# Turning the residual with VectorE and memory instead of TensorE, with the FFN products half a step later

## The chip, the cores and the metric

One core of a Trainium2 chip runs the whole program in one launch. The metric is device time in microseconds (us), the median of several runs. TensorE (PE) does the matmuls, VectorE (DVE), ScalarE (ACT) and GpSimd (POOL) the elementwise work, and SyncE (SP) issues nearly all DMAs.

## The reference

x is 4 x 2048 x 512, fp32. The function is one transformer layer: attention with a causal linear recurrence of 16 heads of 32, then a feed-forward part with low-rank factors. Cut to what matters:

```
x = layernorm(x);  xn = layernorm(x) * ln_g + ln_b
q, k, v = split(xn @ W_qkv + b_qkv);  gate = sigmoid(x @ W_gate + b_gate);  gate /= mean(gate)
q, k = relu(q*gate)**2 + eps, relu(k*gate)**2 + eps
kv[t] = kv[t-1] + k[t] v[t]^T;  ks[t] = ks[t-1] + k[t];  o[t] = (q[t] kv[t]) / (q[t] ks[t] + eps)
x1 = x + o @ W_proj + b_proj
P = layernorm(x1) @ U1;  H = gelu(P @ V1 + b1);  Q = H @ U2;  out = x1 + Q @ V2 + b2
```

U1 is 512 x 128, V1 128 x 2048, U2 2048 x 128, V2 128 x 512.

## The kernel before

The rows of x are cut into 64 chunks of 128 rows (one of the four batches after another at each of 16 positions), and the kernel is a list of 64 steps and a few at the end, written out by `steps(step)` for each engine. In a step (p, b) three chunks are at work: n = chunk b does its projections, c = chunk b-1 its attention and output projection, d = chunk b-2 enters the feed-forward part. Every fp32 product is made of three matmuls, hi by hi, hi by lo and lo by hi (`product`, L849 to L851), so each operand is split by a copy to fp32r (hi) and a subtraction (lo).

The feed-forward part works on groups of two chunks (256 rows), one group for two steps. An odd step (b odd) has the product with U1 (12 matmuls of 256 columns, L959), and pairs 0 to 3 of the eight pairs of 128-row blocks of the hidden layer; the even step that follows has pairs 4 to 7. A pair is an `h_pair` on TensorE (P by V1, 6 matmuls), a `gelu` on ScalarE (L530), an `h_head` on VectorE (the cast h_hi, L665), an `h_tail` on GpSimd (h_lo, L447), and a `q_pair` on TensorE (H by U2, 6 matmuls, added up in ps_q). The odd step also has the result of the group before (`result`, Q by V2).

TensorE's order in a step is: gate; turn of c's queries (`transpose4`, L856); key; turn of d's residual; result (odd only); query; U1 product (odd) or two h pairs (even); scores of c (L980, from key_t and query_t); value; two h pairs (odd only); state of c (L999); outputs of c (L1010, L1016); key sums of n (L1026); two h pairs; y of c (output projection); four q pairs.

VectorE's: gate out of PSUM (L691), gate scale, keys (L653, L656, [x1t_lo L683], L660), results (L716, odd), queries (same lines), pt_lo (L726, odd), block transpose of the keys into zs (L737), probs = scores times the causal mask (L741), values (L749), statistics of a later chunk (L597, L603), state (L767) among two h_heads, ot_lo (L773), zt_lo (L620), two h_heads, key_sums and the denominators (L791 to L805), x1 and its statistics (L815 to L822), zs = normalised x1 (L830), qt_lo (L834, even).

The keys of a chunk are turned without TensorE: VectorE's instruction turns each 32 x 32 block where it stands (L737), SP stores the tile to `blocks_dram` (L351), and four loads of 64 KB, in pieces of 32 elements, put the blocks in their places in `key_t` (L359). The residual of chunk d is in zs; TensorE turns it with four transposes against the identity (L941) into the PSUM bank ps_t, ScalarE copies x1t_hi out (L551) and VectorE makes x1t_lo (L683). The queries are turned in the same way (L926), and stay so.

SP's queue works in the order in which it is written: store results (odd), key_blocks, turned_rows (the means, 4 bytes a row), the four key_t loads, rows, carry_rows, key_sums, xs, xt. It waits at each item for its semaphore, and later items wait behind.

## Time and profile before

| | |
|---|---|
| median of 3 runs | 1702.19 us (1701.56 to 1702.4) |
| the profiled execution | 1701.4 us |
| its span, first to last instruction | 1699.7 us |
| busy: TensorE, VectorE, GpSimd, ScalarE | 1668.6, 1437.1, 880.5, 629.6 us |
| granted TensorE clock, mean | 0.998 |
| chain that ended last | 93% TensorE, 3% VectorE |

Busy time is the union of an engine's instructions. A matmul's shown length (0.39 us for 512 columns) is longer than the distance to the next one, since they overlap: the time that work takes on TensorE is read from the starts.

### The profile page before, as it was taken

How to read it: one execution, taken by the hardware profiler on the slowest of the kernel's cores; microseconds unless marked ns; L12 is line 12 of the kernel's file. 1: busy time of each engine (PE TensorE's matmuls, PEld its weight loads, DVE VectorE, ACT ScalarE, POOL GpSimd, SP SyncE). 2: the span in 40 equal slices, each digit the busy share in tenths (PEclk: the TensorE clock that was granted, in tenths of full speed). 3: DMA queues.
4: the chain of work that ended last, by engine and by line, in shares of the span. 5: the costliest groups of instructions: out<-in, count | busy, mean ns of one | idle time of the engine just before them, and what ended most of it. 6: DMA issues, size and time to landing. Idle time of an engine off the chain costs nothing.

```text
span 1699.7 us, 39613 instructions
## 1 busy us (share of the span) xinstructions
PE 1668.6 (98%) x16221; PEld 1404.5 (83%) x16221; DVE 1437.1 (85%) x2223; ACT 629.6 (37%) x1178; POOL 880.5 (52%) x1026
## 2 busy tenths in 40 slices
PE   6899999999999999999999999999999999999997
PEld 4688888888888888888888888888888888888886
DVE  6888888888888888888888888888888888888885
ACT  4233334333433433433433333333333334334333
POOL 3355555555555555555555555555555555555540
PEclk9999999999999999999999999999999999999999
DMA  8323333333332233242243233333323333323310
GB/s 224 93 58 64 65 75 46 70 75 57 71 70 47 74 71 60 73 64 53 74 72 58 74 46 70 75 59 70 73 45 73 70 60 73 71 47 72 60 45 26
DMA packets 206324, 115.67 MB, mean 68 GB/s; under 512 B 151144, under 2 KB 161792, under 8 KB 206144
## 3 DMA queue, kind: packets, MB, share of 16 engines
q1 hardware_dynamic: 205280, 111.57, 31.6%
q8 instruction: 129, 2.11, 0.7%
q10 hardware_dynamic: 864, 1.57, 0.4%
q14 instruction: 51, 0.42, 0.2%
HBM read 79.38 MB, written 33.72 MB: 67 GB/s over the span
## 4 chain that ended last, share of the span: by engine, by line
PE 93%; DVE 3%; DMA 1%; issue 1%; SPq 1%; ACT 0%; POOL 0%; DVEq 0%; POOLq 0%
PE ps_a L849 11%; PE ps_a L850 10%; PE ps_a L851 10%; PE scores L849 8%; PE scores L851 8%; PE scores L850 8%; PE ps_h L849 4%; PE ps_h L850 4%; PE ps_h L851 4%; PE scores L980 4%; PE scores L1016 4%; PE ps_q L849 3%; PE ps_q L850 3%; PE ps_q L851 3%; PE scores L856 3%; PE scores L1010 2%
## 5 line engine op out<-in xcount | busy, mean ns | idle before, releaser
L447 POOL TENSOR_TENSOR h_lo<-h_full,h_hi 128x512 fp32r<-128x512 f32 x244 | 318.0, 1309 | 233.7 <-DVE h_hi L665 233.7
L849 PE MATMUL ps_a<-wx_hi,zt_hi 128*128 128x512 f32 x768 | 315.7, 411 | 6.6 <-DVE key_sums L787 4.2
L850 PE MATMUL ps_a<-wx_lo,zt_hi 128*128 128x512 f32 x768 | 305.1, 397 | 0.0
L851 PE MATMUL ps_a<-wx_hi,zt_lo 128*128 128x512 f32 x768 | 305.1, 397 | 0.0
L530 ACT ACTIVATE h_full<-ps_h,cols 128x256 f32<-128x256 f32 x512 | 204.0, 475 | 149.7 <-PE ps_h L851 149.6
L665 DVE CAST h_hi<-h_full 128x512 fp32r<-128x512 f32 x256 | 193.5, 766 | 22.9 <-ACT h_full L530 15.8
L849 PEld LDWEIGHTS ps_a<-wx_hi,zt_hi 128*128 128x128 f32 x768 | 145.3, 189 | 43.4 <-DVE zt_lo L620 7.4
L851 PEld LDWEIGHTS ps_a<-wx_hi,zt_lo 128*128 128x128 f32 x768 | 145.1, 189 | 35.6
L850 PEld LDWEIGHTS ps_a<-wx_lo,zt_hi 128*128 128x128 f32 x768 | 145.3, 189 | 28.7 <-issue 0.5
L541 ACT ACTIVATE query_t<-scores 128x512 f32<-128x512 f32 x64 | 38.3, 598 | 345.4 <-PE scores L856 345.4
L401 POOL TENSOR_TENSOR small<-moments,eps_col 128x1 f32<-128x1 f32 x64 | 12.2, 190 | 278.6 <-DVE moments L822 278.6
L849 PE MATMUL ps_h<-pt_hi,v_hi 128*128 128x256 f32 x512 | 144.2, 282 | 1.4 <-DVE pt_lo L726 0.9
L741 DVE TENSOR_TENSOR probs<-scores,causal 128x2048 f32<-128x2048 f32 x64 | 144.1, 2251 | 1.4 <-PE scores L980 1.4
L849 PE MATMUL ps_q<-h_hi,u_hi 128*128 128x256 f32 x512 | 144.8, 283 | 0.4
L850 PE MATMUL ps_h<-pt_lo,v_hi 128*128 128x256 f32 x512 | 144.2, 282 | 0.0
L851 PE MATMUL ps_q<-h_hi,u_lo 128*128 128x256 f32 x512 | 143.7, 281 | 0.0
L850 PE MATMUL ps_q<-h_lo,u_hi 128*128 128x256 f32 x512 | 143.7, 281 | 0.0
L467 POOL TENSOR_TENSOR key_lo<-keys,key_hi 128x512 fp32r<-128x512 f32 x64 | 85.3, 1332 | 112.4 <-ACT key_hi L561 112.4
L851 PE MATMUL ps_h<-pt_hi,v_lo 128*128 128x256 f32 x512 | 143.2, 280 | 0.0
L463 POOL TENSOR_TENSOR keys<-keys,eps_col 128x512 f32<-128x512 f32 x64 | 66.6, 1041 | 123.9 <-DVE keys L660 123.9
L401 POOL TENSOR_TENSOR small<-small,minus_half 128x1 f32<-128x1 f32 x192 | 119.8, 624 | 15.1
L849 PE MATMUL scores<-wx_hi,zt_hi 128*128 128x512 f32 x256 | 106.7, 417 | 0.0
(156 smaller groups left out, 4133.2 us busy)
## 6 DMA issues: line engine op xcount, KB each, us to landing
xs<-L_attn_x SPq DMA_DIRECT2D x64, 256.0 KB, 4.1
key_blocks<-zs SPq DMA_DIRECT2D x64, 256.0 KB, 2.0
key_t<-key_blocks SPq DMA_DIRECT2D x256, 64.0 KB
out<-x1s SPq DMA_DIRECT2D x64, 256.0 KB, 2.1
xt<-x_turned SPq DMA_DIRECT2D x63, 256.0 KB, 4.2
key_sums<-carry_rows SPq DMA_DIRECT2D x60, 256.0 KB, 3.8
rows<-turned_rows SPq DMA_DIRECT2D x63, 64.0 KB, 4.5
x1s<-L_attn_W_gate SPq DMA_DIRECT2D x4, 256.0 KB, 4.1
```

The source lines that it names most:

```text
L401: E.tensor_tensor(out_, a, b, op).then_inc(sem_, 1)
L447: E.tensor_tensor(h_lo[:, i % SLOTS, :], h_full[:, i % SLOTS, :], h_hi[:, i % SLOTS, :].bitcast(F32), ALU.subtract).then_inc(s["h_lo_ready ...
L463: E.tensor_tensor(keys[:, n.half, :], keys[:, n.half, :], eps_wide, ALU.add)\
L467: E.tensor_tensor(key_lo[:, :], keys[:, n.half, :], key_hi[:, :].bitcast(F32), ALU.subtract).then_inc(s["key_lo_ready"], 1)
L530: last = E.activation(h_full[:, i % SLOTS, a * GROUP:(a + 1) * GROUP], ps_h[i % 2][:, a * GROUP:(a + 1) * GROUP], ACT.Gelu_apprx_tanh, bia ...
L665: E.tensor_copy(h_hi[:, i % SLOTS, :], h_full[:, i % SLOTS, :]).then_inc(s["h_hi_ready"], 1)
L741: E.tensor_tensor(probs[:, :, :].rearrange("p j (k t) -> p (j k) t", k=KT), scores[:, :].rearrange("p (g t) -> p g t", g=blocks), causal.u ...
L849: E.matmul(ps, wh, mh, start=start and i == 0, stop=False)
L850: E.matmul(ps, wh, ml, start=False, stop=False)
L851: mm = E.matmul(ps, wl, mh, start=False, stop=stop and i == last)
L980: mm = E.matmul(ps_scores[j][:, ft * P:(ft + 1) * P], key_t[rows, ft, :], query_t[rows, ft, :], start=True, stop=True, tile_position=(HEAD ...
L1016: mm = E.matmul(ps_scores[j][ft * HEAD:(ft + 1) * HEAD, 0:P], values[:, c.half, h * HEAD:(h + 1) * HEAD], probs[:, j, ft * P:(ft + 1) * P] ...
```

## The change

The turn of the residual leaves TensorE and PSUM. VectorE turns zs by 32 x 32 blocks into the queries' buffer right after the gate has left PSUM; SP, first thing in its step, stores that to a new tensor in memory, `res_dram`, waits, and sends four loads back into zs. ScalarE makes x1t_hi from zs, ahead of ot_hi in an odd step and after the last gelu in an even one; VectorE makes x1t_lo ahead of ot_lo in an odd step and after the denominators in an even one. The queries of chunk n wait for that store. The block transpose of the keys now goes to the gate's buffer, and the denominators, which use that buffer, wait for `blocks_out`.

The FFN products are placed anew. The U1 product comes after the key sums of the odd step, and h pairs 0 and 1 at its end. The even step has h pairs 2 and 3 after the gate product, q pairs 0 to 3 with h pairs 4 and 5 after the query product, h pairs 6 and 7 before y, and q pairs 4 to 7 last. The gelus, the h_heads (0 to 3 in a row after the gate) and the h_tails follow.

```
SP, first in its step:
+                d = Chunk(p, b - 2)
+                if d.exists:
+                    sp.wait_ge(s["res_ready"], d.done())
+                    for j in range(HPG):
+                        wait(sp, res_in[j], d.done(16, 16) - 16)
+                    sp.dma_start(res_dram, queries[:, :]).then_inc(s["res_out"], 16)
+                    sp.wait_ge(s["res_out"], d.done(16, 16))
+                    for j in range(HPG):
+                        sp.dma_start(zs[j * HEAD:(j + 1) * HEAD, :].rearrange("d (f a t) -> d f a t", f=KT, t=HEAD),
+                                     res_dram.rearrange("(a d) (f j t) -> j d f a t", d=HEAD, f=KT, t=HEAD)[j])\
+                            .then_inc(res_in[j], 16)
-                    sp.dma_start(blocks_dram, zs[:, :]).then_inc(s["blocks_out"], 16)
+                    sp.dma_start(blocks_dram, gate[:, :]).then_inc(s["blocks_out"], 16)
GpSimd:
+                early_tails = ffn.exists and b % 2 == 0 and not is_last(p)
+                if early_tails:
+                    for i in range(4):
+                        h_tail(ffn, i)
...
+                if early_tails:
+                    add_bias_out()
+                    add_bias(n)
ScalarE:
+                def turned_residual():
+                    if d.exists:
+                        for j in range(HPG):
+                            act.wait_ge(res_in[j], d.done(16, 16))
+                        E.activation(x1t_hi[:, :, d.half * P:(d.half + 1) * P],
+                                     zs[:, :].rearrange("p (k n) -> p k n", k=KT), ACT.Copy)\
+                            .then_inc(s["x1t_hi_ready"], 1)
VectorE:
+                def early_heads():
+                    if ffn.exists and b % 2 == 0:
+                        for i in range(4):
+                            h_head(ffn, i, finishing)
+                def turn_residual():
+                    if d.exists:
+                        dve.wait_ge(s["z1_ready"], d.done())
+                        if c.exists:
+                            dve.wait_ge(s["tq_done"], c.done())
+                        E.transpose(queries[:, :], zs[:, :]).then_inc(s["res_ready"], 1)
...
+                    turn_residual()
+                    early_heads()
...
+                    if d.exists:
+                        dve.wait_ge(s["res_out"], d.done(16, 16))
                     squared_relu(n, s["query_done"], s["query_steps"], ps_a, QUERY, queries[:, :])
...
-                    E.transpose(zs[:, :], keys[:, n.half, :]).then_inc(s["blocks_ready"], 1)
+                    E.transpose(gate[:, :], keys[:, n.half, :]).then_inc(s["blocks_ready"], 1)
...
+                if b % 2:
+                    x1t_tail()
...
+                    dve.wait_ge(s["blocks_out"], n.done(16, 16))
...
+                if b % 2 == 0:
+                    x1t_tail()
TensorE:
+                if ffn.exists and b % 2 == 0:
+                    h_pair(ffn, 2)
+                    h_pair(ffn, 3)
...
-                    transpose4(zs, s["tx_done"])
...
+                    if d.exists:
+                        pe.wait_ge(s["state_ready"], d.done())
+                    for i in range(4):
+                        q_pair(ffn, i)
+                    h_pair(ffn, 4)
+                    h_pair(ffn, 5)
...
-                if ffn.exists and b % 2:
-                    h_pair(ffn, pairs[0])
-                    h_pair(ffn, pairs[1])
...
+                if b % 2 and ffn.exists:
...
+                    pe.wait_ge(s["x1t_ready"], d.done())
+                    wait(pe, s["h_full_ready"], Group(ffn.p, ffn.off - 1).done(PAIRS, PAIRS))
+                    product(ps_h[1][:, 0:GROUP], [(u1_hi[:, k, :], u1_lo[:, k, :]) for k in range(KT)],
+                            [(x1t_hi[:, k, :], x1t_lo[:, k, :]) for k in range(KT)]).then_inc(s["p_done"], 1)
+                if ffn.exists and b % 2 == 0:
+                    h_pair(ffn, 6)
+                    h_pair(ffn, 7)
...
+                if ffn.exists and b % 2:
+                    h_pair(ffn, 0)
+                    h_pair(ffn, 1)
+                if ffn.exists and b % 2 == 0:
...
+                    for i in range(4, 8):
                         q_pair(ffn, i)
```

## Rows read from the trace of the kernel before

**Rows 1.** Windows: length, busy of PE, PEld, DVE, ACT, POOL, clock, DMA share, GB/s

```profile
807.54:834.68 27.14, 27.14 (x265) 23.15 (x264) 23.45 (x36) 9.64 (x18) 13.96 (x17) 1.00 0.35 75
834.68:859.05 24.37, 24.37 (x247) 20.48 (x246) 20.71 (x32) 9.64 (x18) 13.78 (x17) 1.00 0.35 55
```

**Rows 2.** Waits, 400 to 1600 us, TensorE's largest (total, times, longest)

```profile
PEld scores L1016 <- issue: 9.3, 47, 0.2
```

**Rows 3.** Timeline of TensorE around the residual's turn: start, length, instruction

```profile
810.76 0.60 PE L856 MATMUL scores<-ident,zs 128*128 128x128 f32 x4
811.12 0.48 PE L849 MATMUL scores<-v_hi,pt_hi 128*128 128x512 f32 x1
811.43 0.39 PE L850 MATMUL scores<-v_lo,pt_hi 128*128 128x512 f32 x1
```

**Rows 4.** Windows of TensorE alone: query, U1, scores, value, state with outputs and sums

```profile
812.60:815.39 2.79, 2.79 (x14) 1.00 0.68 231
815.39:816.81 1.42, 1.42 (x13) 1.00 0.72 270
816.90:818.00 1.10, 1.10 (x33) 1.00 0.24 93
818.00:820.91 2.91, 2.91 (x17) 1.00 0.24 90
822.42:824.85 2.43, 2.43 (x100) 1.00 0.07 7
```

**Rows 5.** Timeline of VectorE in the same odd step

```profile
811.23 0.75 DVE L653 SCALAR_TENSOR_TENSOR keys<-scores,small,bias 128x512 f32<-128x512 f32 x1
...
815.66 0.75 DVE L653 SCALAR_TENSOR_TENSOR queries<-ps_a,small,bias 128x512 f32<-128x512 f32 x1
...
818.18 0.70 DVE L737 STREAM_TRANSPOSE zs<-keys 128x512 f32<-128x512 f32 x1
818.80 2.25 DVE L741 TENSOR_TENSOR probs<-scores,causal 128x2048 f32<-128x2048 f32 x1
821.11 0.75 DVE L749 SCALAR_TENSOR_TENSOR values<-ps_a,small,bias 128x512 f32<-128x512 f32 x1
...
822.69 0.43 DVE L665 CAST h_hi<-h_full 128x512 fp32r<-128x512 f32 x1
...
823.42 1.34 DVE L665 CAST h_hi<-h_full 128x512 fp32r<-128x512 f32 x1
```

**Rows 6.** Timeline of SP's queue: xt, and key_t behind turned_rows and without it

```profile
811.55 0.43 SPq L285 DMA_DIRECT2D xt<-x_turned  x1
...
823.13 3.25 SPq L359 DMA_DIRECT2D key_t<-key_blocks  x4
...
1619.07 2.61 SPq L359 DMA_DIRECT2D key_t<-key_blocks  x4
```

**Rows 7.** DMA issues: count, KB each, median us from issue to landing

```profile
key_blocks<-zs SPq DMA_DIRECT2D x64, 256.0 KB, 2.0
...
xt<-x_turned SPq DMA_DIRECT2D x63, 256.0 KB, 4.2
```

**Rows 8.** DMA view, 811 to 818 us: busy tenths in 40 slices

```profile
DMA  0001354445777499999974320006999999930000
```

**Rows 9.** The same view, 1619 to 1625 us

```profile
DMA  0000000001797169742599237873000100000000
```

**Rows 10.** The same view, 823 to 835 us

```profile
DMA  0110000422403959950010435302000096319000
```

**Rows 11.** Timeline at the end: the last zs, its split and its U1 product

```profile
1674.24 0.55 DVE L830 TENSOR_SCALAR zs<-x1s,moments,small 128x512 f32<-128x512 f32 x1 [0.93 <-POOL small L401]
...
1675.54 0.60 ACT L551 ACTIVATE x1t_hi<-scores 128x512 fp32r<-128x512 f32 x1 [0.64 <-PE scores L856]
...
1676.17 0.69 DVE L683 TENSOR_TENSOR x1t_lo<-scores,x1t_hi 128x512 fp32r<-128x512 f32 x1 [0.81 <-ACT x1t_hi L551]
...
1676.92 0.38 PE L849 MATMUL ps_h<-x1t_hi,u_hi 128*128 128x256 f32 x1
```

More of the change, by code:

```diff
@@ L215, in block_kernel @@
         xt_in = [sem(f"xt_in{i}") for i in range(4)]
+        res_in = [sem(f"res_in{j}") for j in range(HPG)]
         key_t_in = [sem(f"key_t_in{j}") for j in range(HPG)]
@@ L469, in step @@
                 center(Chunk(p, b + 1))
-                if ffn.exists and not is_last(p):
-                    h_tail(ffn, pairs[0])
-                    h_tail(ffn, pairs[1])
-                    h_tail(ffn, pairs[2])
-                    h_tail(ffn, pairs[3])
+                if early_tails:
+                    for i in range(4, 8):
+                        h_tail(ffn, i)
                 if c.exists:
@@ L537, in step @@
                 ffn = Group(p, (b - 3) // 2) if b % 2 else Group(p, (b - 4) // 2)
-                pairs = range(4) if b % 2 else range(4, 8)
+                def turned_residual():
[6 more added lines that the diff above has]
+                if ffn.exists and b % 2 == 0:
+                    gelu(ffn, 2)
+                    gelu(ffn, 3)
+                if n.exists:
+                    act.wait_ge(s["gate_evac"], n.done())
+                    E.activation(gate[:, :], gate[:, :], ACT.Sigmoid, accum_out=gate_sum[:, :])\
+                        .then_inc(s["gate_sig"], 1)
                 if c.exists:
@@ L675, in step @@
                 ffn = Group(p, (b - 3) // 2) if b % 2 else Group(p, (b - 4) // 2)
-                pairs = range(4) if b % 2 else range(4, 8)
                 finishing = is_last(p)
@@ L768, in step @@
                                     ALU.add).then_inc(s["state_ready"], 1)
-                if ffn.exists and b % 2:
-                    h_head(ffn, pairs[1], finishing)
+                if b % 2:
+                    x1t_tail()
                 if c.exists:
@@ L775, in step @@
                 z_tail(Chunk(p, b + 1))
-                if ffn.exists:
-                    h_head(ffn, pairs[2], finishing)
-                    h_head(ffn, pairs[3], finishing)
+                if b % 2 and ffn.exists:
+                    dve.wait_ge(s["pt_hi_ready"], ffn.done())
+                    E.tensor_tensor(pt_lo[:, :], ps_h[1][:, 0:GROUP], pt_hi[:, :].bitcast(F32), ALU.subtract)\
+                        .then_inc(s["pt_ready"], 1)
+                if ffn.exists and b % 2 == 0:
+                    h_head(ffn, 6, finishing)
+                    h_head(ffn, 7, finishing)
                 if n.exists:
@@ L908, in step @@
                 result = Group(p, (b - 5) // 2) if b % 2 else None
-                pairs = range(4) if b % 2 else range(4, 8)
                 if n.exists:
@@ L952, in step @@
                     project(QUERY, ps_a, s["query_done"])
-                if b % 2 and ffn.exists:
-                    if isinstance(p, int) and p == 0:
-                        pe.wait_ge(s["stage_lo"], len(tiles))
-                    pe.wait_ge(s["x1t_ready"], d.done())
-                    wait(pe, s["h_full_ready"], Group(ffn.p, ffn.off - 1).done(PAIRS, PAIRS))
-                    product(ps_h[1][:, 0:GROUP], [(u1_hi[:, k, :], u1_lo[:, k, :]) for k in range(KT)],
-                            [(x1t_hi[:, k, :], x1t_lo[:, k, :]) for k in range(KT)]).then_inc(s["p_done"], 1)
-                if ffn.exists and b % 2 == 0:
-                    h_pair(ffn, pairs[0])
-                    h_pair(ffn, pairs[1])
+                if ffn.exists and b % 2 == 0:
+                    if d.exists:
[4 more added lines that the diff above has]
+                    h_pair(ffn, 5)
                 if c.exists:
@@ L989, in step @@
                     project(VALUE, ps_a, s["value_done"])
-                if ffn.exists and b % 2:
-                    h_pair(ffn, pairs[0])
-                    h_pair(ffn, pairs[1])
                 if c.exists:
@@ L1038, in step @@
                             [(wp_hi[:, k, :], wp_lo[:, k, :]) for k in range(KT)]).then_inc(s["y_done"], 1)
-                if ffn.exists:
+                if ffn.exists and b % 2:
+                    h_pair(ffn, 0)
+                    h_pair(ffn, 1)
+                if ffn.exists and b % 2 == 0:
                     if c.exists:
                         pe.wait_ge(s["state_ready"], c.done())
-                    for i in pairs:
+                    for i in range(4, 8):
                         q_pair(ffn, i)
@@ L1070 @@
     blocks_dram = nc.dram_tensor("key_blocks", (P, DM), _mybir.dt.float32, kind="Internal").ap()
+    res_dram = nc.dram_tensor("residual_blocks", (P, DM), _mybir.dt.float32, kind="Internal").ap()
     rows_dram = nc.dram_tensor("turned_rows", (BATCHES, P), _mybir.dt.float32, kind="Internal").ap()
-    block_kernel(nc, *args, out, carry_dram, rows_dram, blocks_dram)
+    block_kernel(nc, *args, out, carry_dram, rows_dram, blocks_dram, res_dram)
     r = _run(nc, [arrays], core_ids=[0])
```

93 lines of the change are left out of this document (32 added, 61 removed).

## The prediction

> **What bounds the kernel now.** I read the share of each engine over one odd and one even step first, then the table of waits, then the order of work inside one odd step, engine by engine. The two windows [rows 1] run from the turn of the queries in one step to the same point in the next: TensorE is busy for all of 27.14 us in the odd step and all of 24.37 in the even one. A pair of steps is 51.51 us. The waits on TensorE's side between 400 and 1600 us are only small ones put down to "issue" [rows 2], so no other engine holds it up. VectorE is busy 23.45 and 20.71 us of the same windows: second, but not far behind. TensorE's granted clock is 1.00, the 2.4 GHz level, in both windows. So what leaves TensorE is gained only if the engines behind it keep the new, shorter pace, and the question is asked step by step, because the change also makes the two kinds of step unequal.
>
> **What leaves TensorE.** The four turns of zs, once a step. Their slot is 810.76 to 811.12, 0.36 us, and the product behind them needs 0.31 to its second matmul where 0.23 is the pace (2.79 us for twelve) [rows 3, 4]; 0.43 us a step, 0.86 a pair. The Trainium skill (TensorE: Matmul & The Clock Gate, Part 4: PE-mode transpose) gives about 275 ns for a turn inside a kernel, which by its figure would be 1.1 us a step, an estimate of 70 us for the kernel. The trace has 0.60 us for four that overlap, and the slot in it is what counts.
>
> **What moves.** A half of the second-factor work (four q pairs) and two h pairs go from the odd to the even step. A product of twelve 256-column matmuls takes 1.42 us [rows 4], a pair has six, 0.71. So six pairs are 4.26 us. TensorE's own work becomes 27.14 - 0.43 - 4.26 = 22.45 in the odd step and 24.37 - 0.43 + 4.26 = 28.20 in the even step, 50.65 together: if all is covered, 0.86 us a pair is gained.
>
> **The odd step, walked through.** I keep the clock of the step that begins at 807.54. Without the turns the query product (2.79) ends at 815.0. The product with U1, that stood behind it (1.42), is now after the sums. So the scores run 815.1 to 816.2 (1.10), the value product to 819.1 (2.91), and the state products to 819.65 (some 0.46 of the 2.43 us that they, the output products and the sums take together) [rows 4]. There the output products want probs.
>
> VectorE cannot be so early. It takes the queries out of PSUM when their product is done and then has its chain: from 815.66 to the start of probs at 818.80 are 3.14 us, of which 0.34 is pt_lo, which moves away; and probs takes 2.25 [rows 5]. From 815.3 (VectorE reaches it at 814.7 to 815.3, since keys at 811.23 and what follows move up by the x1t_lo that leaves, and get the new transpose in the time that it spent waiting for the gate) that makes 815.3 + 2.80 + 2.25 = 820.35, 0.75 late. Before, two h pairs and the U1 product (2.84) lay in TensorE's way to this point and covered it.
>
> The second place is the U1 product. TensorE without waits would be at it at 819.65 + (2.43 - 0.46) = 821.6 [rows 4]. It needs x1t_lo, which VectorE now makes behind values, the statistics and the state: 1.58 from values to the end of the statistics [rows 5], some 0.4 for the state (an estimate: a quarter of the columns of values), 0.69 for itself [rows 11]; 820.4 + 2.7 = 823.1. So by here the odd step is 1.5 us late in all (the 0.75 is in it). Behind it the y product (its ot_lo is made by 823.8) and h pairs 0 and 1 (pt_lo while y runs) are covered; nothing gives the 1.5 back.
>
> **The transfers.** The turned residual leaves from the queries' buffer, and the queries may not be written before it has left. SP reaches the new store only behind xt, issued at 811.55 [rows 6], so at 812.0. Alone a store of this size lands 2.0 us later [rows 7], at 814.0, which would be in time. But key_sums, xs and xt are in flight and their packets keep the DMA engines at 7 to 9 tenths up to about 814.8 [rows 8]; xt lands 4.2 us after its issue [rows 7], at 815.75, and the two result stores behind it fill 1.3 us, 815.75 to 817.05 [rows 8], 0.65 each. In order behind xt the store lands at 816.35. VectorE wants the buffer at 815.3: 1.05 us late, with 0 (store alone) as the lower bound. I take 1.05, as the rows show queued transfers there. It delays queries and probs alike, and so adds to the 1.5: 2.55 a pair. In the even step the transposed residual is ready later and the early heads lie ahead of the queries: covered.
>
> The four loads into zs are of the kind of key_t: 128-byte packets. Where no turned_rows store is ahead of them, their packets are through by about 1623.8, 4.7 us after the first issue [rows 6, 9]; behind turned_rows they last to some 833.4, 10.3 us [rows 6, 10]. The new ones go behind a big store, so I take the short form: 816.35 + 4.7 = 821.1 to 822, ScalarE's copy 0.6 [rows 11], done before VectorE's 822.4. Covered, by little. If they take 10.3 it is the rival below. key_blocks is sent about a microsecond later in the step than now, when SP has issued the four loads (816.35 + 3.25 = 819.6); its reader is in the next step. It goes out of the gate buffer, which is written again only at the denominators.
>
> **The even step.** VectorE's work is 20.71 busy plus 0.62 for the transpose (818.18 to 818.80) plus four heads of 0.43 (port free) to 1.34 us (GpSimd in its own subtraction) [rows 5], 1.7 to 5.4; with the 3.66 us in which it was not busy in this step [rows 1] that is 26.7 to 30.4 against TensorE's 28.2. Early heads come in pairs that slip through between GpSimd's tails, so I take about 3.8 for the four: 28.8, and the waits among the 3.66 shrink (the gate's sigmoid of up to 1.7 is now covered). I put nothing down for it and keep up to 2.2 for the range.
>
> **The end.** The last residual has no next step to hide in. Now zs is written at 1674.24 to 1674.79 and the U1 product starts at 1676.92 [rows 11], 2.1 us. After: transpose 0.7, store 2.0 and 0.3 to notice it, loads 4.7, copy 0.6, x1t_lo 0.69, and some 0.1 between each: 9.3. Plus 7. If the loads are of the long form it is 5.6 more.
>
> **Sum.** 31 full pairs. -0.86 x 31 = -27; +2.55 x 31 = +79; +7 at the end. 1701.4 + 59 = 1760; the median of the runs shown is 1702.2, so the same figure stands for it. With the store alone (0 instead of 1.05) it is 1728.
>
> **Rivals.**
> 1. All covered: TensorE keeps the pace, 1701.4 - 27 + 7 = 1681. For it: TensorE has no wait now, VectorE is under 90%. Against: the chain query, probs, output is counted from rows and is longer than what TensorE has left beside it; it decides if VectorE gets from the query product to probs' end in less than 4.6 us.
> 2. A draw: the delays in the odd step are only about the 0.86 gained, 1700 to 1705.
> 3. The residual's loads take as long as key_t's now. They land at 816.35 + 10.3 = 826.7, ScalarE stands at its wait with ot_hi behind it, x1t_lo is ready at 828.1 instead of 824.1: 4.0 a pair more, +124, 1885. It sets in when the loads take over 6.5 us. The Trainium skill (DMA: Bandwidth & Descriptors, the table at its head) wants 512 B a descriptor for line rate, which speaks against any plan with 128-byte pieces; both kinds of rows above have them, so it does not choose between 4.7 and 10.3.
> 4. VectorE becomes the bound of the even step too: +2.2 x 31 = +68, 1828. The Trainium skill (SBUF — State Buffer, Who interferes with whom) says that a copy of VectorE in its fast mode and a GpSimd instruction exclude each other for their whole length. By that rule, the trace agrees: 1.34 against 0.43 for the same cast.
>
> **Chances.** The odd step's delays outweigh the gain (1706 to 1810): 0.61. All or nearly all covered: 0.16. Draw: 0.06. Slow loads: 0.07. Even step too: 0.10. Range 1690 to 1810: it leaves out most of rival 1 and rival 3 and a part of rival 4; the likeliest case alone is 1725 to 1790. No change can be told from one of 0.2%, 3.4 us. Faster 0.16, same 0.06, slower 0.78.
>
> **What would show it.** In the trace after: TensorE waiting at the output products for probs, at the value product for queries, and at the U1 product for x1t_lo, all in odd steps, each around 1 us; VectorE waiting for a DMA into residual_blocks ahead of the queries; pairs of about 53.2 us; even steps near 28.2; ScalarE with a short or no wait for zs. The forecast is wrong if odd steps are 22.5 long (VectorE quicker than counted), if ScalarE waits for zs by 4 us and more, or if VectorE never idles in the even steps and these are 30 long.

## The result, and the profile after

| | before | after |
|---|---|---|
| median (runs, range) | 1701.9 us (4, 1701.6 to 1702.4) | 1845.0 us (4, 1835.4 to 1855.1) |
| ratio, 95% interval | | 1.083 (1.080 to 1.086) |
| profiled execution, its span | 1701.4, 1699.7 us | 1855.1, 1853.3 us |
| a pair of steps, behind the first | 51.51 us, always | 54.3 to 60, mean 56.0 us |
| last turn of the queries to the end | 42.8 us | 57.9 us |

The change is a loss of 8.3%: 85 us more than forecast, and 35 above the upper end of the range. The four runs stand in two pairs, near 1836 and near 1854 us, and the profiled one is the longest, so the trace below has 154 us to explain where the medians have 143. Three parts make the 154 us between the two spans: 8 us up to the fifth turn of the queries, 130 us from there to the last one, 15 us at the end. The page of the kernel after shows the change of character first: the engines' busy times, and the chain that ended last, which was 93% TensorE before.

```profile
PE 1694.7 (91%) x15965; PEld 1402.0 (76%) x15965; DVE 1511.8 (82%) x2291; ACT 625.5 (34%) x1178; POOL 921.7 (50%) x1022
...
DMA 49%; DVE 26%; PE 14%; issue 5%; SPq 5%; ACT 1%; DVEq 0%; POOL 0%; POOLq 0%; ACTq 0%
...
residual_blocks<-queries SPq DMA_DIRECT2D x64, 256.0 KB, 4.8
zs<-residual_blocks SPq DMA_DIRECT2D x256, 64.0 KB, 2.5
```

VectorE is busy for 75 us more, of which its 64 new transposes of 0.70 explain 45; GpSimd is busy for 41 us more with four instructions fewer. Something makes instructions longer. The two windows that answer to [rows 1], an odd step and the even one behind it:

```profile
916.47:944.64 28.17, 25.70 (x238) 20.77 (x237) 20.72 (x35) 7.34 (x15) 10.07 (x18) 0.94 0.41 89
944.64:972.58 27.94, 26.84 (x268) 22.91 (x267) 25.47 (x35) 11.79 (x22) 19.33 (x17) 1.00 0.37 69
```

From turn to turn TensorE's own work is 23.87 us odd (the 22.45 of the forecast, which counts from gate to gate, with the 1.42 of two h pairs) and 26.78 even. The odd step has 4.3 us over that, the even one 1.2. TensorE is no longer busy throughout, and in the odd step its granted clock is 0.94. The waits between 400 and 1600 us, to be held against [rows 2]:

```profile
ACT x1t_hi L564 <- DMA zs<-residual_blocks: 126.8, 21, 7.7
...
DVE queries L682 <- DMA residual_blocks<-queries: 68.2, 38, 3.5
...
PE scores L1031 <- DVE probs L776: 53.5, 33, 2.4
...
PE ps_a L885 <- DVE queries L682: 29.1, 15, 2.7
```

Two chains hold TensorE: the queries wait for the store in nearly every step (38 of 43), and the output products wait for probs in odd and even steps alike. Added up by kind of step, TensorE's matmuls wait 2.5 us in an odd step and 1.5 us in an even one, on the mean between 400 and 1600 us.

**The odd step.** SP's queue first ([rows 6] show xt before), then VectorE ([rows 5]):

```profile
921.35 0.43 SPq L286 DMA_DIRECT2D xt<-x_turned  x1
921.96 0.33 SPq L348 DMA_DIRECT2D residual_blocks<-queries  x1
926.76 2.62 SPq L351 DMA_DIRECT2D zs<-residual_blocks  x4
```

```profile
926.82 0.75 DVE L682 SCALAR_TENSOR_TENSOR queries<-ps_a,small,bias 128x512 f32<-128x512 f32 x1 [3.30 <-DMA residual_blocks<-queries]
927.61 0.75 DVE L685 SCALAR_TENSOR_TENSOR queries<-queries,gate_scale,gate 128x512 f32<-128x512 f32 x1
928.39 0.69 DVE L689 SCALAR_TENSOR_TENSOR queries<-queries 128x512 f32<-128x512 f32 x1
929.00 0.70 DVE L772 STREAM_TRANSPOSE gate<-keys 128x512 f32<-128x512 f32 x1
929.63 2.25 DVE L776 TENSOR_TENSOR probs<-scores,causal 128x2048 f32<-128x2048 f32 x1
```

The store lands 4.8 us after its issue, and VectorE stands 3.30 us before it touches the queries. From there to probs it takes 2.81 us, which is the 2.80 of the forecast. So it is, within 0.1 us, in 13 of the 21 odd steps; in the other 8 (most of them between 1140 and 1490 us) it takes 3.0 to 4.8 us, and there TensorE waits up to 2.35 us for probs instead. TensorE's value product, which writes the bank that the queries are read from, waits:

```profile
927.63 0.74 PE L885 MATMUL ps_a<-wx_hi,zt_hi 128*128 128x512 f32 x1 [2.47 <-DVE queries L682]
```

Behind such a wait comes the second loss. This window of the same step shows the granted clock at 0.50, the 1.2 GHz level, while TensorE is busy all the time:

```profile
927.72:931.13 3.41, 3.41 (x8) 2.67 (x9) 3.38 (x4) 0.00 (x0) 0.00 (x0) 0.50 0.64 134
```

It issues 8 matmuls in 3.41 us there, where the 2.4 GHz level has 0.23 us for each. Such a stretch is called a fall below. The whole trace has 27 of them, 108.5 us together (before: 2, 9.6 us, none between 400 and 1600). Each of the 16 between 400 and 1600 us begins 1.8 to 4.0 us behind the start of a wait of TensorE's matmuls of 1.9 to 2.6 us; 9 more waits of 1.8 us and over had none behind them. At half the rate 108.5 us cost at most 54, and at most 49 more than the falls of before.

**The even step.** Here the forecast put nothing down. VectorE's chain, and GpSimd beside it:

```profile
953.64 0.75 DVE L682 SCALAR_TENSOR_TENSOR queries<-ps_a,small,bias 128x512 f32<-128x512 f32 x1 [0.40 <-DMA residual_blocks<-queries]
954.42 1.71 DVE L685 SCALAR_TENSOR_TENSOR queries<-queries,gate_scale,gate 128x512 f32<-128x512 f32 x1
956.17 1.67 DVE L689 SCALAR_TENSOR_TENSOR queries<-queries 128x512 f32<-128x512 f32 x1
957.76 0.70 DVE L772 STREAM_TRANSPOSE gate<-keys 128x512 f32<-128x512 f32 x1
958.39 2.25 DVE L776 TENSOR_TENSOR probs<-scores,causal 128x2048 f32<-128x2048 f32 x1
```

```profile
954.31 1.28 POOL L475 TENSOR_TENSOR x1s<-x1s,bias_out 128x512 f32<-128x512 f32 x1
955.55 1.74 POOL L450 TENSOR_TENSOR xs<-xs,bias_proj 128x512 f32<-128x512 f32 x1
957.25 1.74 POOL L490 TENSOR_TENSOR key_lo<-keys,key_hi 128x512 fp32r<-128x512 f32 x1
```

The same two multiplications of the queries take 1.71 and 1.67 us in place of 0.75 and 0.69, so the chain is 4.75 instead of 2.81. Their ends show how: 954.42 + 1.71 = 956.13 is 0.54 behind the end of GpSimd's addition (954.31 + 1.28 = 955.59), and 956.17 + 1.67 = 957.84 is 0.55 behind the next one's (957.29). VectorE's instruction gets through only when GpSimd's is over, and GpSimd's next one, held in turn, takes 1.74 instead of 1.28. In this step TensorE waits 1.10 us at the output products for probs.

The price could have been read before. In the kernel before, the same engines meet at another place (groups of VectorE, 400 to 1600 us: busy time, mean ns of one):

```profile
L794 DVE SCALAR_TENSOR_TENSOR gate<-queries,key_sums 128x512 f32<-128x512 f32 x46 | 59.1, 1286 | 1.6
L660 DVE SCALAR_TENSOR_TENSOR queries<-queries 128x512 f32<-128x512 f32 x47 | 32.5, 692 | 1.6
```

Both have two tensors of SBUF as inputs. The first runs beside GpSimd's h_tails and takes 1.29 us on the mean; the second ran beside nothing and took 0.69. The Trainium skill (SBUF — State Buffer, Who interferes with whom) says that a VectorE instruction with two SBUF inputs contends with a GpSimd instruction that reads SBUF, and that the later one of them is blocked until the other ends. By that rule, the trace agrees, in both directions. The forecast used the same section for the casts only.

### The profile page after: what moved, and what is told of

Read it like the earlier page. It is cut to its first block, busy times and chain, and to the rows that moved or that the text cites. A ratio compares the mean times of both kernels' runs of the same rounds, so it can differ in the third digit from the quotient of the medians.

```text
span 1853.3 us, 39585 instructions
## 1 busy us (share of the span) xinstructions
PE 1694.7 (91%) x15965; PEld 1402.0 (76%) x15965; DVE 1511.8 (82%) x2291; ACT 625.5 (34%) x1178; POOL 921.7 (50%) x1022
## 3 DMA queue, kind: packets, MB, share of 16 engines
q10 hardware_dynamic: 864, 1.57, 0.3%
## 4 chain that ended last, share of the span: by engine, by line
DMA 49%; DVE 26%; PE 14%; issue 5%; SPq 5%; ACT 1%; DVEq 0%; POOL 0%; POOLq 0%; ACTq 0%
DMA turned_rows<-small 23%; DMA residual_blocks<-queries 15%; DMA carry_rows<-key_sums 11%; DVE probs L776 4%; DVE queries L689 4%; DVE queries L685 3%; DVE queries L682 3%; DVE h_hi L694 2%; PE ps_a L885 2%; DVE stats L626 2%; DVE values L784 2%; PE ps_a L887 2%; PE ps_a L886 2%; DVE gate L772 1%; SPq L283 1%
## 5 line engine op out<-in xcount | busy, mean ns | idle before, releaser
L460 POOL TENSOR_TENSOR h_lo<-h_full,h_hi 128x512 fp32r<-128x512 f32 x240 | 335.4, 1421 | 134.3 <-DVE h_hi L694 134.3
L885 PE MATMUL ps_a<-wx_hi,zt_hi 128*128 128x512 f32 x768 | 320.6, 417 | 54.4 <-DVE queries L682 48.0
L887 PE MATMUL ps_a<-wx_hi,zt_lo 128*128 128x512 f32 x768 | 311.8, 406 | 0.0
L886 PE MATMUL ps_a<-wx_lo,zt_hi 128*128 128x512 f32 x768 | 311.6, 406 | 0.0
L694 DVE CAST h_hi<-h_full 128x512 fp32r<-128x512 f32 x256 | 169.3, 702 | 16.1 <-ACT h_full L551 15.9
L887 PEld LDWEIGHTS ps_a<-wx_hi,zt_lo 128*128 128x128 f32 x768 | 149.1, 194 | 37.1
L886 PEld LDWEIGHTS ps_a<-wx_lo,zt_hi 128*128 128x128 f32 x768 | 149.8, 195 | 31.4 <-issue 0.5
L592 ACT ACTIVATE ot_hi<-scores 128x512 fp32r<-128x512 f32 x64 | 38.4, 599 | 270.8 <-PE scores L1037 270.8
L682 DVE SCALAR_TENSOR_TENSOR queries<-ps_a,small,bias 128x512 f32<-128x512 f32 x64 | 48.0, 750 | 98.9 <-DMA residual_blocks<-queries 96.3
```

The lines of the kernel that those rows point to most:

```text
L460: E.tensor_tensor(h_lo[:, i % SLOTS, :], h_full[:, i % SLOTS, :], h_hi[:, i % SLOTS, :].bitcast(F32), ALU.subtract).then_inc(s["h_lo_ready ...
L682: E.scalar_tensor_tensor(out=dst, in0=ps[:, :], scalar=small[:, n.slot, 4:5], in1=bias[:, group, :], op0=ALU.mult, op1=ALU.add).then_inc(c ...
L694: E.tensor_copy(h_hi[:, i % SLOTS, :], h_full[:, i % SLOTS, :]).then_inc(s["h_hi_ready"], 1)
L885: E.matmul(ps, wh, mh, start=start and i == 0, stop=False)
L886: E.matmul(ps, wh, ml, start=False, stop=False)
L887: mm = E.matmul(ps, wl, mh, start=False, stop=stop and i == last)
```

## The experiments

All ratios are to the kernel before, run beside it on the same chip. The step lengths are from turn to turn of the queries, means between 400 and 1600 us, and falls are the stretches at half clock in the same part, in the profiled execution.

| | edit | median us (range) | ratio, 95% | odd, even step | falls |
|---|---|---|---|---|---|
| | changed kernel | 1845.0 | 1.083 (1.080, 1.086) | 27.46, 28.88 | 16 |
| e1 | residual leaves from another buffer | 1822.3 (1815 to 1824) | 1.069 (1.067, 1.071) | 28.28, 26.78 | 14 |
| e2 | store issued ahead of xs and xt | 1793.3 (1791 to 1797) | 1.053 (1.052, 1.055) | 27.40, 26.77 | 19 |
| e6 | e1 and e2 | 1822.9 (1819 to 1832) | 1.069 (1.067, 1.071) | 28.61, 26.78 | 18 |
| e3 | new FFN placement alone | 1815.6 (1807 to 1821) | 1.064 (1.061, 1.068) | 27.20, 27.73 | 4 |
| e4 | filler products in the waits | 1841.8 (1839 to 1844) | 1.082 (1.080, 1.083) | 27.30, 28.12 | 0 |
| e8 | changed kernel, GpSimd held back | 1809.7 (1804 to 1813) | 1.062 (1.059, 1.064) | 27.17, 27.24 | 8 |
| e5 | e3, GpSimd held back | 1757.9 (1758 to 1760) | 1.032 (1.031, 1.034) | 25.37, 27.73 | 0 |
| e7 | e6, GpSimd held back | 1733.6 (1730 to 1737) | 1.018 (1.016, 1.020) | 25.35, 26.78 | 0 |
| e9 | e7, GpSimd and x1t_lo in a new order | 1719.3 (1717 to 1721) | 1.010 (1.008, 1.011) | 24.69, 26.77 | 0 |
| e12 | e9, keys turned behind values in odd steps | 1710.4 (1709 to 1714) | 1.005 (1.003, 1.006) | 24.54, 26.78 | 0 |
| e10 | before, key_hi ahead of pt_hi | 1723.8 (1722 to 1724) | 1.012 (1.010, 1.014) | 27.93, 24.36 | 0 |
| e11 | before, GpSimd held back | 1701.8 (1700 to 1704) | 1.000 (0.999, 1.001) | 27.14, 24.37 | 0 |

**e1, the store's wait taken away.** The turned residual goes to the half of `values` that is free until the value product of the step, so the queries wait for no store.

```
-                        if c.exists:
-                            dve.wait_ge(s["tq_done"], c.done())
-                        E.transpose(queries[:, :], zs[:, :])
+                        E.transpose(values[:, d.half, :], zs[:, :])
...
-                    if d.exists:
-                        dve.wait_ge(s["res_out"], d.done(16, 16))
                     squared_relu(n, s["query_done"], ...)
...
                     dve.wait_ge(s["value_done"], n.done())
+                    if d.exists:
+                        dve.wait_ge(s["res_out"], d.done(16, 16))
```

> The residual's blocks leave from the half of values that is free at that time, so the queries no longer wait for the store. Theory 1 (that wait is the largest loss of the odd steps, and the fall of TensorE's clock behind it is its second half): VectorE's 96 us of waiting for the store go, odd steps shorten from 26.5-28.2 us to about 25.4, the clock falls in odd steps vanish, 1765 to 1790 us in all against 1845. Theory 2 (VectorE's own chain to probs and x1t_lo is the loss and the store only coincides with it): not under 1825 us.

The time is in neither theory's range. The wait for the store is gone and the even step is at its floor of 26.78, but the odd step grew to 28.28. In the odd step of this kernel the queries start early, and GpSimd's subtraction now falls on them (VectorE's timeline):

```profile
920.86 1.79 DVE L685 SCALAR_TENSOR_TENSOR queries<-queries,gate_scale,gate 128x512 f32<-128x512 f32 x1
922.69 1.66 DVE L689 SCALAR_TENSOR_TENSOR queries<-queries 128x512 f32<-128x512 f32 x1
```

TensorE waits 2.3 us for probs in each of the 22 odd steps, long enough for falls of the clock. The wait for the store had kept the queries out of GpSimd's way: taking it away alone swapped one loss for another.

**e2, the store ahead of xs and xt.** SP issues residual_blocks first and then the loads of xs and xt (whose call stood at the end of the step before).

```
                     sp.dma_start(res_dram, queries[:, :]).then_inc(s["res_out"], 16)
+                load_x(Chunk(p, b + 2))
+                if d.exists:
                     sp.wait_ge(s["res_out"], d.done(16, 16))
```

> SP issues the residual's store before xs and xt of the same step instead of behind them; all else as in the changed kernel. Theory 1 (the store lands 4.8 us after its issue because two loads of 256 KB are ahead of it in the queue): it lands 2.0 to 2.8 us after its issue, VectorE's wait falls from 96 us to under 20, 1765 to 1795 us. Theory 2 (the landing is slow whatever is ahead, from the memory's side): landing stays above 4 us and the time at 1835 to 1855 us.

VectorE's waits for the store fell from 68.2 to 10.7 us between 400 and 1600, and the time by 52, as theory 1 had it: the store's place behind the two loads was worth that much. But it lands 3.8 us after its issue (median) and not 2.0 to 2.8, with the load of key_sums, issued about 1 us before, still ahead of it. The odd step did not move, since with the queries no longer held by the store GpSimd meets them: the second multiplication takes 1.58 us on the mean in odd steps (0.97 in the changed kernel), and TensorE waits up to 2.1 us for probs in each of 22.

**e6, both.**

> The changed kernel with both edits on the store: from the free half of values, and issued ahead of xs and xt. Theory 3: the store's wait is gone already with either edit (1822 and 1793), so little is gained over 1793; the wait for probs stays at about 2.3 us a pair: 1785 to 1800 us. Theory 1 (the transfers are the larger loss): under 1770 us.

Missed by 23 us: no wait for the store, no better than e1, and 30 us slower than e2. The odd step is 28.61, the multiplications 1.79 and 1.67 us. In e2 the store still delayed the queries in 11 of 22 odd steps, the first multiplication took 1.01 us on the mean, and TensorE waited 1.95 us for probs; here it waits 2.34. Where the store still holds the queries back, less is lost to the collision: the transfers are not what is left.

**e3, the FFN placement alone.** TensorE turns the residual as before, and the rest of the change stays: U1 product behind the sums, h pairs and q pairs, gelus, early heads and tails, keys turned into the gate's buffer.

```
-                    turn_residual()
+                    x1t_tail()
...
+                    transpose4(zs, s["tx_done"])
...
-                                     zs[:, :].rearrange("p (k n) -> p k n", k=KT), ACT.Copy)
+                                     ps_t[:, :].rearrange("p (k n) -> p k n", k=KT), ACT.Copy)
```

> Only the new placement of the FFN products, with TensorE's turn of the residual as before and no residual transfers. Theory 1 (the placement alone takes TensorE's cover from VectorE's chain to probs in the odd step, 0.75 us, and from the even step about 1.2 us): 1702 + 31 x (0.75 to 2) = 1725 to 1765 us, with TensorE waiting for probs at the output products. Theory 2 (the placement is harmless, the loss is all from the transfers and the longer VectorE list): 1700 to 1710 us.

114 us slower without a single byte of the new transfers, and 50 above the range of theory 1. VectorE's timeline and TensorE's wait in one odd step:

```profile
932.89 1.33 DVE L669 SCALAR_TENSOR_TENSOR queries<-queries,gate_scale,gate 128x512 f32<-128x512 f32 x1
934.26 1.67 DVE L673 SCALAR_TENSOR_TENSOR queries<-queries 128x512 f32<-128x512 f32 x1
```

```profile
938.77 0.51 PE L1020 MATMUL scores<-query_t,state 32*32 32x128 f32 x32 [2.28 <-DVE probs L757]
```

Why did this not happen before? ScalarE's and GpSimd's timelines of the kernel before, in the odd step of [rows 5]:

```profile
817.01 0.38 ACT L556 ACTIVATE pt_hi<-ps_h 128x256 fp32r<-128x256 f32 x1 [5.01 <-PE ps_h L851]
817.29 0.62 ACT L561 ACTIVATE key_hi<-keys 128x512 fp32r<-128x512 f32 x1
```

```profile
817.99 1.29 POOL L467 TENSOR_TENSOR key_lo<-keys,key_hi 128x512 fp32r<-128x512 f32 x1 [2.55 <-ACT key_hi L561]
```

ScalarE stood 5.01 us at its wait for the U1 product, with key_hi behind it, and GpSimd's key_lo, which needs key_hi, started only at 817.99, when the queries' multiplications (from 815.66 on) were over. With the U1 product moved to the step's end that wait is gone, key_hi is early, and key_lo and the centring run right beside the queries. The change removed an unwritten order between two engines.

**e4, filler.** Eight and five unused products a pair are put into TensorE's waits (their results go to a bank that is written again), to see whether the clock falls follow the waits: ahead of the value product in odd steps, behind the state products in even ones.

```
+                    filler(Group(ffn.p, ffn.off - 1), PAIRS, 8)
                     pe.wait_ge(s["query_steps"], n.done(3, 1))
...
+                        filler(ffn, PAIRS - 3, 5)
```

> The changed kernel with 13 products more for each pair of steps, whose result is not used: 8 of 512 columns ahead of the odd step's value product and 5 ahead of the even step's output products, where TensorE waits anyway 2.5 and 1.1 to 2.5 us. They compute nothing of the output. Theory 1 (the clock falls only behind TensorE's waits of over 2 us, and each fall costs 1.7 us): mean granted clock from 0.971 to 0.99 or more, 1800 to 1815 us although there is more work. Theory 2 (clock falls have another cause): clock unchanged, 1845 us or up to 3 us a pair more.

No fall between 400 and 1600 us, and steady pairs of 55.4 us, but the time is nearly that of the change and not the 1800 to 1815 expected: 13 products of some 0.23 us are 3.0 us a pair, and TensorE still waits 1.1, which is together about the 4.0 that it waited in the changed kernel. It shows that the falls come with the waits. It does not give their price.

**e5, e7 and e8, GpSimd held back.** One wait more on GpSimd, ahead of key_lo, the centring and, in even steps, the bias additions:

```
                         .then_inc(s["key_ready"], 1)
+                    pool.wait_ge(s["query_steps"], n.done(3, 3))
```

> The placement alone (1815.6 us), and GpSimd waits for the queries' third instruction before the key_lo, the center and, in even steps, the two bias additions. Theory 3 (the placement brings GpSimd's reads into VectorE's queries chain, whose two instructions with SBUF inputs grow from 0.75 and 0.69 us to 1.3 to 1.7 and 1.67, and TensorE waits for probs 2.3 us for that): they fall back to 0.75 to 0.8 and 0.69, the wait for probs in odd steps to about 0.8, pairs from 54.65 to about 52.5, 1735 to 1755 us. Theory 1 (the missing cover of 2.84 us alone): the instructions' length is a result of something else and the time stays within 1800 to 1820.

> As the one before, and GpSimd waits for the queries' third instruction. Theory 3: the queries' instructions fall to 0.75 and 0.69, the odd step's wait for probs from 2.3 to about 0.8 us, fewer or no clock falls, pairs of about 52.3, 1730 to 1750 us. If the residual's loads are what holds the odd step by then (x1t_lo), 1760 to 1780 us.

> The changed kernel, only GpSimd waits for the queries' third instruction. In its odd steps the late store keeps the queries clear of GpSimd for the most part, so the odd step keeps its loss; the even step's wait for probs (1.2, and 2.5 in the steps with a clock fall) goes: even steps of 26.8, no falls in even steps. Theory 3: 1785 to 1815 us against 1845. Theory 1: 1835 to 1855.

A wait that only delays one engine makes e3 faster by 58 us, e6 by 89 and the changed kernel by 35. e7 and e8 are in the ranges of theory 3, e5 is 3 us above its own. In e5 and e7 no fall is left between 400 and 1600 us, the multiplications of the odd step are back at 0.75 and 0.69, and the odd step has the same 25.35 us whoever turns the residual. e8 gains less, since there the queries still wait for the store (60.5 us between 400 and 1600); its 8 falls are all in odd steps, as expected, but its even steps are 27.24 and not 26.8. The two transfer edits, worth 22 us without the wait (e6), are worth 76 with it (e8 to e7). In e7 three waits are left in an odd step (TensorE's, and its weight load's, timelines):

```profile
929.74 1.17 PE L1005 MATMUL scores<-query_t,key_t 32*128 32x128 f32 x32 [0.68 <-DVE x1s L760]
934.62 0.51 PE L1032 MATMUL scores<-query_t,state 32*32 32x128 f32 x32 [0.34 <-DVE probs L775]
936.86 0.19 PEld L886 LDWEIGHTS ps_h<-x1t_hi,u_hi 128*128 128x128 f32 x1 [0.49 <-DVE x1t_lo L714]
```

0.68 + 0.34 + 0.49 = 1.51, and 25.35 - 23.87 = 1.48. The sum is the forecast's 1.5 us for the cover that moved away, but the places are not: it had no wait ahead of the scores, and 0.75 at each of the other two.

**e10 and e11, the collision in the kernel before.** e10 exchanges two lines of ScalarE in odd steps, and nothing else:

```
-                if b % 2 and ffn.exists:
-                    act.wait_ge(s["p_done"], ffn.done())
-                    E.activation(pt_hi[:, :], ps_h[1][:, 0:GROUP], ACT.Copy)...
                 if n.exists:
                     act.wait_ge(s["key_ready"], n.done())
                     E.activation(key_hi[:, :], keys[:, n.half, :], ACT.Copy)...
+                if b % 2 and ffn.exists:
+                    act.wait_ge(s["p_done"], ffn.done())
+                    E.activation(pt_hi[:, :], ps_h[1][:, 0:GROUP], ACT.Copy)...
```

> The kernel before, with one exchange: in odd steps ScalarE makes key_hi ahead of pt_hi. That lets GpSimd subtract key_lo and centre from about 816.1 to 818.7 on the clock of the step that begins at 807.54, beside the queries' two multiplications, instead of from 817.99. If the collision is the cause of the longer chain, these multiplications take 1.3 to 1.7 us instead of 0.75 and 0.69, and probs starts 1.0 to 1.7 later. TensorE has two h pairs and the U1 product as cover at this place (2.84 us), so the time should stay at 1702 to 1706 and no clock fall should come. If the collision is not the cause, the multiplications stay at 0.75 and 0.69. If the collision costs time whatever the cover, 1702 + 31 x 1.5 = 1748.

> The kernel before with the wait that was given to GpSimd in the other versions: key_lo and the centring only after the queries' chain. Control: if what the wait gained elsewhere was the collision that the change brought in, it gains nothing here: the odd and even steps stay at 27.14 and 24.37, 1702 within 3 us. If it is a gain in any order of work, the time falls below 1698.

The multiplications went from 0.75 and 0.69 to 1.58 and 1.67 us, beside GpSimd's two instructions (VectorE, then GpSimd):

```profile
929.96 1.58 DVE L656 SCALAR_TENSOR_TENSOR queries<-queries,gate_scale,gate 128x512 f32<-128x512 f32 x1
931.57 1.67 DVE L660 SCALAR_TENSOR_TENSOR queries<-queries 128x512 f32<-128x512 f32 x1
```

```profile
929.71 1.28 POOL L467 TENSOR_TENSOR key_lo<-keys,key_hi 128x512 fp32r<-128x512 f32 x1 [0.74 <-ACT key_hi L558]
930.95 1.74 POOL L428 TENSOR_TENSOR xt<-xt,rows 128x512 f32<-128x512 f32 x1
```

Here too VectorE's instructions end 0.55 us behind GpSimd's. The cause is shown by itself: an exchange of two copies of ScalarE brings the collision and 22 us. My expectation of no cost was wrong: 2.84 us of cover keep TensorE from waiting for probs, but VectorE is late behind probs as well, and the y product then waits for ot_lo in each odd step (0.42 us on its matmuls, 0.6 on its weight load). The odd step is 0.79 longer; where the rest of that goes is not shown. No wait is over 1 us, and no fall comes. The control e11 gives nothing, so the held GpSimd is no gain by itself; it only mends what the placement broke.

**e9 and e12, how far the idea goes.** e9: in odd steps GpSimd's two bias additions go behind the centring (the keys' multiplication took 1.57 us beside them in e7), and VectorE makes x1t_lo right behind values. e12: in odd steps VectorE turns the keys behind values instead of ahead of probs.

```
GpSimd (e9):
                 center(Chunk(p, b + 1))
+                if not early_tails:
+                    add_bias_out()
+                    add_bias(n)
VectorE (e12), behind values:
+                if n.exists and b % 2:
+                    turn_keys()
                 if b % 2:
                     x1t_tail()
```

> The version with both transfer edits and GpSimd held back (1733.63) with two places in the order changed: in odd steps GpSimd's two bias additions go behind key_lo and the centring, and VectorE makes x1t_lo right after values. In that version an odd step of 25.35 us holds three waits of TensorE: scores for the results' evacuation 0.68, output products for probs 0.34, U1 product for x1t_lo 0.49, 1.51 together. The keys' multiplication took 1.57 instead of 0.75 beside GpSimd's bias addition. If the theory is right (the only cost left is VectorE's chain, lengthened by GpSimd's two-input reads, and x1t_lo), the multiplication falls to 0.75, the three waits all but go, the odd step is 23.9 to 24.3, the pair 50.65 to 51.1, and the time 1733.6 - 31 x (1.05 to 1.5) = 1687 to 1701. If the turn through memory has another cost of its own in the odd step, it stays at 25.0 or more and the time at 1722 or more.

> The version with GpSimd's new order (1719.28), with one more move: in odd steps VectorE turns the keys' blocks behind values instead of ahead of probs. In that version TensorE's only wait of an odd step is 0.73 us at the output products, for probs, and a pair is 51.48. The keys' turn takes 0.62 out of the way to probs, and VectorE stands idle at the place where it goes, since x1t_lo waits there for the residual's loads. If VectorE's way from the query product to probs is what holds the odd step, that wait falls to 0.1 to 0.2, a pair is 50.8 to 50.95 and the time 1719.3 - 31 x 0.6 = 1701, a draw with the kernel before: the 0.86 us a pair that left TensorE is then nearly all there (22 us of 27), and the end of the kernel, 15 us longer than before, takes most of it. If the later store of the keys' blocks makes a new wait (denominators or key_t), the pair stays at 51.3 or more.

In e9 one wait of an odd step is left, 0.73 us at the output products; the pair is 51.48, above the 50.65 to 51.1 expected, and the time 18 us above the range. In e12 the odd and the even step, and the two waits left (totals of 24):

```profile
911.54:936.07 24.53, 24.39 (x237) 19.66 (x236) 21.55 (x37) 7.33 (x15) 11.40 (x19) 1.00 0.44 101
936.07:962.86 26.79, 26.79 (x269) 22.93 (x268) 24.13 (x34) 11.81 (x22) 17.01 (x14) 1.00 0.35 72
```

```profile
PEld ps_h L889 <- DVE x1t_lo L714: 10.6, 24, 0.5
...
PEld scores L1035 <- DVE probs L776: 5.9, 24, 0.2
```

51.32 less 0.44 and 0.25 is 50.63: the 50.65 of the forecast for TensorE's work is there. The wait for probs went as expected, but x1t_lo took its place (ScalarE has x1t_hi only at 924.65, since the residual's loads land at 924.0, and x1t_lo then starts at 924.90 behind the keys' turn and takes 0.99 us beside a bias addition of GpSimd), so e12 won 9 us and not 18. It is the fastest kernel with the change, and 0.5% slower than before: from the fifth turn of the queries to the last it is 8.6 us shorter than before, its start is 3.8 longer, and its end 15.3.

**The end.** From the last turn of the queries to the last instruction: 42.8 us before, 50.3 in e5 (placement alone), 57 to 59 in all kernels with the turn through memory. TensorE's waits after 1795 us in the changed kernel, of which the first two are one wait:

```profile
PEld ps_h L885 <- DVE x1t_lo L711: 7.3, 1, 7.3
...
PE ps_h L885 <- DVE x1t_lo L711: 6.9, 1, 6.9
```

## Why the prediction was wrong

It had the sign (0.78 for slower) and most mechanisms, and the size at 59 us instead of 143. The steps that failed are the length of VectorE's chain from the query product to probs, taken as fixed, and the even step, put at nothing; the clock that fell behind the longer waits was not in the sum at all. A pair was forecast 2.55 us over TensorE's own 50.65 and is 5.7 over it (27.46 + 28.88): 2.5 are TensorE's waits in the odd step, 1.5 its waits in the even step, 1.4 what the half clock takes from both, and 0.3 is not traced. The odd step's 2.5 is the forecast's 2.55 in size only: it is 1.4 at the value product, for the queries, and 1.0 at the output products, with next to nothing at the U1 product, and the store and the collision take turns in it. Step by step:

**TensorE's work, -27: right.** 50.65 a pair was forecast and is in e12 once its waits are taken off; the even step's floor of 26.78 is 28.20 less two h pairs.

**The cover that moves away, 1.5 a pair: right in sum, in part by luck.** The forecast had 0.75 at the output products and as much again at the U1 product. e7 has 1.51 in all, of which 0.68 is a wait for the results that the forecast did not have, behind a keys' multiplication of 1.57 us beside GpSimd (0.75 in e9). e9, where that one is gone, has 0.73 at the output products alone, but x1t_lo is made earlier there, so no run measures the second 0.75 by itself. That part of the sum, 1701.4 - 27 + 46 + 7 = 1728, stands against e7's 1733.6, whose end is 7.5 us longer than the sum has it.

**"1.05 us late" for the store: right mechanism, mis-sized.** It was 3.30 in the step shown. On the step's own clock the store was issued at 5.49 us instead of 4.46 (xt itself at 4.88 instead of 4.01), took 4.8 us instead of 4.35, and the queries wanted the buffer at 7.05 instead of 7.76, since VectorE got to them earlier than counted. Three errors of 0.45 to 1.0 us, all of one sign, on a difference of two large numbers. On the mean VectorE waits 2.0 us for the store in an odd step and 1.2 in an even one, where it was called covered.

**"815.3 + 2.80": the step that failed.** The length of the chain from queries to probs was taken from the kernel before as if it belonged to the instructions. It belongs to them and to what GpSimd does meanwhile: 2.81 us where GpSimd is out of the way, 4.4 to 4.8 in the odd steps of e3, e1 and e6, where it reads SBUF beside the two multiplications. The forecast moved the U1 product and followed what waits for it, but not what had been standing behind it on ScalarE: pt_hi's wait held key_hi, and so held key_lo. In the changed kernel's own odd steps the late store hid this failure in 13 of 21; it shows as soon as the store's wait is taken away (e1, e2, e6).

**"The even step: I put nothing down": failed by the same mechanism.** The forecast added up how long VectorE is busy and did not follow its chain. The casts' burst was 3.58 us against 3.8 forecast; it is the chain behind them that was longer, 4.75 us in the step shown and 4.4 on the mean against 2.84 before, and the step is 2.1 us over its floor of 26.78 (1.5 waits, 0.6 half clock). Rival 4 had the lock between VectorE and GpSimd, and its price of 2.2 us was near, but at the casts, and as a question of VectorE's throughput; VectorE was busy 25.47 of 27.94 us there and idle in between, so it was late, not full.

**The clock: not in the forecast.** Behind waits of TensorE of 1.8 us and more come stretches of 3.4 us at half clock, in many steps though not in all (e3 has 22 waits of up to 2.3 us and 4 falls). That is at most 49 us of the 154 in the trace. e4, which fills the waits, has none of them.

**The end, +7: half of it.** The turn through memory costs its 7 us (zs is written by 1818.89, x1t_lo ready at 1827.95: 9.1 us against 9.3 forecast). The placement costs 7.5 more (e5), which no step counted.

**The loads: right.** They are of the short form (the last lands 4.4 to 4.9 us after the first issue), and x1t_lo never waits for them in the odd steps of the changed kernel. Rival 3 did not come. Its sign did: ScalarE waits up to 7.7 us for zs, but the late store is in that wait as well, so the sign could not tell one from the other.

**Two slips in the working.** 820.35 - 819.65 is 0.70 and not 0.75, which changes nothing. Rival 3 sets x1t_lo's 828.1 against 824.1, where the walk has 823.1: by the walk that rival costs 5.0 a pair and not 4.0.

Along one path the 85 us that were missed are: GpSimd's collision in the changed kernel 35 (after to e8), the store beyond its forecast 1.05 a pair 43 (76 from e8 to e7, less 33), and 6 in e7 itself against 1728. These are differences of medians. On another path the shares differ, since each loss hides a part of the other: the transfer edits alone win 22, GpSimd's wait alone 35, both together 111. How much of each share is the fall of the clock and how much the wait before it, these runs don't separate.

## What to carry to other kernels

When an instruction is moved away, list what stood behind it on every engine that waits for it: a wait that costs nothing may be all that keeps two other engines from meeting. The length of a VectorE instruction with two SBUF inputs is not a constant: look in the trace for the same form beside GpSimd and alone, and price a chain by both. And a removed wait is judged only together with what it lets start earlier; here the same edit was worth 22 or 76 us, depending on one semaphore of GpSimd.

## What the runs showed of the hardware

A multiplication of 128 x 512 fp32 with both inputs in SBUF took 0.69 to 0.75 us alone and 1.3 to 1.9 beside additions and subtractions of GpSimd, with its end 0.54 to 0.56 us behind the end of GpSimd's instruction in every one over 1.2 us between 400 and 1600 us (48 in the changed kernel, 65 in e1, 88 in e3, 46 in e10; the 46 of L794 in the kernel before as well); GpSimd's took 1.74 instead of 1.28 when it came second. Every fall to a granted clock of 0.50 between 400 and 1600 us of the changed kernel (3.4 us each, one twice that) began 1.8 to 4.0 us behind the start of a wait of TensorE's matmuls of 1.9 to 2.6 us; not every such wait had one (4 falls on 22 waits of up to 2.3 us in e3, 14 on 22 in e1), and e4, e5, e7, e9, e10 and e12, where no wait of its matmuls is over 0.8 us, had none. A store of 256 KB landed 4.8 us after its issue (median) with three loads of the same size still under way (key_sums, xs, xt, in the changed kernel), 3.8 us with key_sums alone ahead of it (e2), and 2.0 us with none (key_blocks, in the kernel before).
